# Attention with latent projections and a mixture of experts on eight cores: the softmax denominator's reciprocal moves from VectorE to ScalarE, and the output accumulator gets a second PSUM bank

## The reference

```
q_lat, k_lat, v_lat = x @ Wq_down, x @ Wk_down, x @ Wv_down      # 16 heads of 64
q, k = concat(lat @ Wup_c, rope(lat @ Wup_e)); v = v_lat @ Wv_up
att = softmax(causal(q k^T / 8));  y = att @ v                   # per head
x = layernorm(x + y @ Wc)
g = top-2 softmax gate over 8 experts
x = layernorm(x + sum_e g_e * (silu(x W1_e) * (x W2_e)) W3_e)    # hidden 2730
```

## Time and profile before

| | us |
|---|---|
| median of 2 runs | 7562.65 (7557.54 and 7567.77) |
| the profiled execution | 7564.37, its span 7562.8 |
| spans of the 8 cores | 7455.5 to 7562.8 |
| attention on core 5 | about 600 to 2128 |
| experts and last norm on core 5 | about 2475 to 7562 |

### The profile page before, as it was taken

The page is one execution under the profiler, slowest core; times in us unless marked ns, Lnnn a source line. Parts: engine busy times, 40 slices in busy tenths (PEclk is TensorE's granted clock), DMA queues, the critical chain, the costliest instruction groups (busy, mean ns, idle before and its releaser), DMA issues.

```text
span 7562.8 us, 58931 instructions; the slowest of 8 cores (7455.5 to 7562.8 us)
## 1 busy us (share of the span) xinstructions
PE 5336.2 (71%) x20398; PEld 2012.1 (27%) x20398; DVE 1586.5 (21%) x2608; ACT 756.6 (10%) x947; POOL 620.9 (8%) x1151
## 2 busy tenths in 40 slices
PE   5666645544643887778777787778877778788883
PEld 1221111111111333333333333333333333333331
DVE  3552211111244111111111111111111111111114
ACT  0002211211200000000000000000000001000000
POOL 1011111110000000000001000100000000000000
PEclk7665555555566999999999999999999999987897
DMA  5258999995010443333333343333433334333342
GB/s 86 45 103 182 211 199 193 200 206 118 2 43 29 115 117 113 106 113 114 111 107 110 110 117 113 110 104 113 117 109 109 111 111 117 111 104 99 105 117 92
DMA packets 928042, 868.15 MB, mean 115 GB/s; under 512 B 62976, under 2 KB 786176, under 8 KB 927504
## 3 DMA queue, kind: packets, MB, share of 16 engines
q1 hardware_dynamic: 790448, 528.55, 22.9%
q0 software_dynamic: 137312, 335.83, 22.2%
HBM read 866.32 MB, written 146.80 MB: 134 GB/s over the span
## 4 chain that ended last, share of the span: by engine, by line
DMA 44%; PE 39%; issue 7%; DVE 6%; ACT 2%; DVEq 0%; POOL 0%; SPq 0%; POOLq 0%; ACTq 0%
PE pS L839 31%; DMA w12s<-w12b 17%; DMA w3s<-w3b 13%; PE px L839 9%; DMA w12b<-wtb 4%; DMA wtb<-w12i 4%; DMA wtb<-w3p 3%; DMA w3b<-wtb 2%; ACT attTA L839 1%; DVE rbuf L839 1%; DVE rzs L839 1%; DVE cbuf L839 1%; DVE oac L839 1%; DMA wstage<-wq 1%; DVE lnm L839 1%
## 5 line engine op out<-in xcount | busy, mean ns | idle before, releaser
L839 PE MATMUL pS<-uA,w12s 128*128 128x512 bf16 x5632 | 1369.0, 387 | 381.4 <-DMA w12s<-w12b 318.3
L839 PE MATMUL pS<-x1te,w12s 128*128 128x512 bf16 x5632 | 1358.0, 385 | 0.0
L839 PE MATMUL pS<-w3s,hiddenG 128*128 128x512 bf16 x2816 | 762.2, 395 | 627.4 <-DMA w3s<-w3b 584.1
L839 DVE TENSOR_TENSOR hiddenG<-s1b,pS 128x512 bf16<-128x512 bf16 x704 | 483.9, 687 | 2352.1 <-PE pS L839 2352.1
L839 ACT ACTIVATE s1b<-pS 128x512 bf16<-128x512 f32 x704 | 420.3, 597 | 4536.6 <-PE pS L839 4536.6
L839 PEld LDWEIGHTS pS<-uA,w12s 128*128 128x128 bf16 x5632 | 521.0, 99 | 1198.4 <-issue 720.4
L839 PE MATMUL px<-w3s,hiddenG 128*128 128x512 bf16 x2816 | 762.4, 395 | 0.0
L839 POOL DMA_DIRECT2D w3s<-w3b x704 | 378.7, 538 | 4631.8 <-PE px L839 4518.2
L839 PEld LDWEIGHTS pS<-x1te,w12s 128*128 128x128 bf16 x5632 | 558.0, 99 | 687.8 <-issue 86.3
L839 PEld LDWEIGHTS pS<-w3s,hiddenG 128*128 128x128 bf16 x2816 | 243.5, 99 | 1122.2 <-issue 965.2
L839 PE MATMUL px<-attTA,V 128*65 128x512 bf16 x640 | 289.6, 604 | 310.2 <-DVE ytmp L839 254.0
(11 more groups left out here) (92 smaller groups left out, 1619.0 us busy)
## 6 DMA issues: line engine op xcount, KB each, us to landing
w12s<-w12b SPq DMA_DIRECT2D x704, 512.0 KB, 4.1
w3s<-w3b POOLq DMA_DIRECT2D x704, 256.0 KB, 2.9
wtb<-w12i POOLq DMA_DIRECT2D x234, 384.0 KB, 8.5
w12b<-wtb SPq DMA_DIRECT2D x234, 384.0 KB, 6.3
wtb<-w3p POOLq DMA_DIRECT2D x117, 384.0 KB, 8.5
w3b<-wtb SPq DMA_DIRECT2D x117, 384.0 KB, 6.3
xres<-x SPq DMA_DIRECT2D x16, 512.0 KB, 3.5
out<-outb SPq DMA_DIRECT2D x16, 512.0 KB, 2.6
```

The lines of the kernel that those rows point to most:

```text
L839: inst = getattr(engine, meth)(*a, **k)
```

## The change

```diff
 def emit_y(h, qS, g, nkc, m_exp):
+        yb = 4 + (h * 4 + qS) % 2
...
         if g == 0:
-            S.bank_wait("tensor", 4)
+            S.bank_wait("tensor", yb)
...
-            my = S.op("tensor", "matmul", pf[4][0:65, :],
+            my = S.op("tensor", "matmul", pf[yb][0:65, :],
...
-            bb = 5 + ((h * 4 + qS) % 2)
-            S.wait("vector", "sp", m_ylast)
-            S.slot_wait("vector", ("rzs",))
-            mrz = S.op("vector", "reciprocal", rzs[64:65, 0, :],
-                       pf[4][64:65, :], inc="sv")
-            S.wait("tensor", "sv", mrz)
+            upar = (h * 4 + qS) % 2
+            yb = 4 + upar
+            bb = 6 + upar
+            S.wait("scalar", "sp", m_ylast)
+            S.slot_wait("scalar", ("rzs",))
+            S.op("scalar", "activation", rzs[64:65, 0, :],
+                 pf[yb][64:65, :], AF.Ln)
+            S.edge("scalar", "ss")
+            mrz = S.op("scalar", "activation", rzs[64:65, 0, :],
+                       rzs[64:65, 0, :], AF.Exp, scale=-1.0, inc="ss")
+            S.wait("tensor", "ss", mrz)
...
                            A5[0:64, hp, qS * 512:(qS + 1) * 512],
-                           pf[4][0:64, :], bsb[0:64, 0, :], inc="sv")
+                           pf[yb][0:64, :], bsb[0:64, 0, :], inc="sv")
...
                 mtt = S.op("vector", "tensor_mul", ytmp[0:64, qS % 2, :],
-                           pf[4][0:64, :], bsb[0:64, 0, :], inc="sv")
+                           pf[yb][0:64, :], bsb[0:64, 0, :], inc="sv")
...
-            S.bank_free(4, "sv", mtt)
+            S.bank_free(yb, "sv", mtt)
```

## The result

| | us |
|---|---|
| changed kernel, median of 22 runs | 7481.13 (7444.23 to 7698.38) |
| kernel before, median of 21 runs beside them | 7650.57 (7532.82 to 7822.86) |
| ratio | 0.9885, interval 0.9862 to 0.9909 |
| predicted | 7495, range 7440 to 7535, ratio of the sum 0.991 |

The medians also hold runs in which a die ran at a lower clock, which is why they lie further apart than the ratio, which leaves such runs out. It says 1.15% faster, 0.9 to 1.4. But it gave 0.95 to "no change that can be told", and the runs tell this one from none. That statement was wrong.

A forecast was written before the change was run, and what follows sets the result against it. Attention was taken as bound by the weight transcode's DMA from 712 to 1805 us, then by its own chain; 11 + 20.5 + 30.9 + 7 = 69.4 us off 7564.37 gives 7495, range 7440 to 7535.

The forecast's parts named there:

- The chain: Attention iteration's tail: logarithm and exponential on ScalarE, together 1.3 us, replace DVE's 3.355 us reciprocal, gaining 2.06 us.
- the pause: TensorE standing still between an iteration's last V product and its broadcast matmul: 3.78 us before, about 1.7 us forecast.
- The second bank: Second accumulator bank: worth nothing in undisturbed iterations; where a multiplication waits for a `ytmp` DMA, TensorE stops one iteration later.
- the release: Near the transcode's end, when multiplications held up by `ytmp` DMAs can run; every listed wait after it was taken as met.
- The start: SP's first `ytmp` DMAs wait for early attention iterations; with five shorter chains, the transcode's end moves 11 us earlier.
- The lead: At the transcode's end, attention in the changed kernel is nearly one iteration further on: 20.5 us.
- The end: After the transcode, 15 chains from (12, 1) to (15, 3) each gain 2.06 us: 30.9 us.
- The clock: Attention after the transcode: less full clock falls on idle TensorE, worth 0 to 14.5 us, taken as 7.
- The clock does not stay up: Rival: in attention's last stretch the shorter idle time keeps TensorE's clock up, giving 7431 us; chance 0.11.
- loads do not appear: Rival: ScalarE loads a table before each logarithm and exponential, giving 7578 us, or 7609 by the skill; chance 0.04.
- the ends do shift: Rival: transcode's end does not move and the lead is lost; only last chains and clock count, 7526 us; chance 0.10.
- The chances: Whole kernel: no change that can be told 0.95, faster by over 2% 0.03, slower by over 2% 0.02.

The follow-up runs named there:

- act_only: Changed kernel with one accumulator bank, keeping logarithm and exponential on ScalarE: ratio 0.9866 to the kernel before.
- bank_only: Changed kernel with the reciprocal back on DVE, keeping two accumulator banks: ratio 0.9959 to the kernel before.
- after_late: Changed kernel with the weight transcode moved behind the attention: ratio 1.1088 to the kernel before, median 8346 us.
- again: The changed kernel itself run once more, unedited, beside its two halves: ratio 0.9875 to the kernel before.
- after_third: The changed kernel once more, unedited, on one chip with a rerun of the kernel before: ratio 0.9859.
- after_actq: Changed kernel with the `ytmp` DMAs on ScalarE's queue in place of SP's: ratio 0.9518 to the kernel before, median 7157.8 us.

## Why the prediction was right, and where wrong

- **The chain.** 2.06 us predicted; 589 + 627 ns for 0.60 each, the pause 1.71 us for 3.78. Right. The row with the same number of columns was the right neighbour, though it has 128 lanes for one.
- **The second bank** is worth nothing in undisturbed iterations. `act_only` and `bank_only` bear it out: in their last 14 intervals, 255.6 and 288.6 us, the bank makes no difference (256.0 to 256.5 and 288.6 to 288.7 in the kernels with the same reciprocal), and what it brings comes at the release.
- **The start.** 11 us predicted; on one chip the start is 11.4 us shorter and the transcode's last load 11.3 earlier, and the transcode took as long from there on.
- **The lead.** 20.5 us predicted, 20.7 between the two slowest cores, but 18.2 on the mean over eight. The path was right. The size was that of core 5, whose multiplication had hardly waited for its DMA; most cores have less to gain.
- **The end.** 15 chains, 30.9 us; with the lead 51.4, measured 51.7. That these agree without the clock term is luck in part: the lead was over 2 us too long, and the 15 chains with their clock are 2.32 us each, 35 us.
- **The clock.** 7 us predicted. This term of the sum was mis-sized. The last 14 intervals shrank by 2.32 us each on the mean where the pause gives 2.07, and `after_late` has 0.26 us per tail beyond the pause: both make 4 us over fifteen. The full clock does fall on work now, but its mean there is 0.53: what the full clock gives back is about half of what I carried over. Whether such stretches are fewer or shorter I have not counted.
- **The rivals.** The clock does not stay up, loads do not appear, the ends do shift.
- **The chances.** This is the step that failed: "about what a measurement of this kernel can tell from no change", put at 2%. No row stood behind that figure; the two runs that I had lay 0.14% apart. The interval of the runs is 0.24% to either side here, and their 1.15% is almost five times that. A sum of 69 us, 0.9%, whose own range did not reach zero, was a forecast of faster, and I had written it down as no change that can be told.

The sum was 69 us, the traces of one chip give 63 at the output projection and 65 on the mean of the cores at full clock, and the ratios correspond to 87 to 106 us. The sum reckoned one core's path and put at nothing what happens to the distance between the slowest core, which sets the time, and the mean. Cores at a clock of 0.834 to 0.842, which some of the runs of both kernels hold, do not explain it. I took only executions in which no core is at 0.845 or below. On the chip of `again` that leaves four of the kernel before and three of the changed one: the mean of the eight cores falls from 7466.3 to 7394.5 us, by 72, and the time from 7510.9 to 7422.7, by 88. On the chip of `after_third` seven and three are left, with 69 and 78 us. So the cores on the mean gain close to the sum, and the slowest one 9 to 16 us more: in these runs the cores lie closer together in the changed kernel. Why they do stays open, and whether they do is not sure: single times of one kernel in this comparison lie up to 64 us apart (7376.85 and 7440.88).

## What to carry to other kernels

Find the stretches in which the changed chain is the limit before multiplying its gain by the number of iterations: here 20 of 64 chains counted, and one edit of a DMA's queue freed the rest. A small DMA whose completion a compute engine needs should not stand in a queue behind bulk transfers that wait for their own loads. And a second buffer brings its lead only when nothing else of the next iteration is queued behind the blocked instruction.

## What I had not expected of the hardware

A one-row instruction of 512 columns costs ScalarE as much as one on 128 rows (589 and 627 ns against 598), which I had assumed, but the two differ: the logarithm out of PSUM takes 38 ns less than the exponential out of SBUF. No run here tells whether the function or the source makes that difference. And full DMA traffic costs the attention's compute next to nothing: 1133.2 us in `after_actq` beside 213 GB/s, 1123.3 in `after_late` with the DMA engines at rest.
